# Attention row maxima: for 5 of 16 query tiles, two key blocks share one maximum through their difference

## The reference, cut to what matters

```python
# (2, 2048, 256); 16 heads of width 16
Q = (x @ WQ + bQ).reshape(b, n, N_HEADS, D_K)
K = (x @ WK + bK).reshape(b, n, N_HEADS, D_K)
V = (x @ WV + bV).reshape(b, n, N_HEADS, D_K)
Qr = jnp.einsum('bnhd,dr->bnhr', Q, WQr)
Kr = jnp.einsum('bnhd,dr->bnhr', K, WKr)
scores = jnp.einsum('bnhr,bmhr->bnhm', Qr, Kr) / math.sqrt(RANK)
A = jax.nn.softmax(scores, axis=-1)
out = jnp.einsum('bnhm,bmhv->bnhv', A, V).reshape(b, n, d)
return out @ WO + bO
```

## Time and profile before

| | |
|---|---|
| Time, median of 3 runs | 2819.9 us (2819.66 to 2824.02) |
| Time of the profiled execution | 2823.65 us |
| Its span | 2821.7 us |
| Attention in the span | about 124 to 1476 us |
| Busy: PE, DVE, ACT | 2386.1, 2258.6, 1691.3 us |

### The profile page before, as it was taken

One profiled execution on the slowest core, in us unless ns is written; L12 is line 12 of the kernel. 1 busy time (PEld: TensorE's weight loads), 2 busy tenths in 40 slices (PEclk: granted clock), 3 DMA queues, 4 the chain that ended last, 5 costly groups with the idle time before them and its releaser, 6 DMA issues. The chain is left out here.

```text
span 2821.7 us, 45555 instructions
## 1 busy us (share of the span) xinstructions
PE 2386.1 (85%) x14814; PEld 1060.6 (38%) x14814; DVE 2258.6 (80%) x3705; ACT 1691.3 (60%) x3462; POOL 961.9 (34%) x729
## 2 busy tenths in 40 slices
PE   8898999999999999999986799917476676679991
PEld 5322222222222222222225478812122222357881
DVE  7898999999999999999924844428799999785443
ACT  3347888888888888888881433306556556443330
POOL 4500000000000000000020277772499999426772
PEclk9879999999999999999997799957799999879996
DMA  4505111111111111111145469981234333245997
GB/s 152 145 24 177 43 34 50 50 36 40 50 50 36 40 50 50 32 44 50 28 132 186 142 162 270 234 124 28 55 112 113 105 112 110 85 142 153 272 239 204
DMA packets 255163, 293.69 MB, mean 104 GB/s; under 512 B 39120, under 2 KB 210448, under 8 KB 254928
## 3 DMA queue, kind: packets, MB, share of 16 engines
q1 hardware_dynamic: 213664, 235.09, 28.7%
q0 software_dynamic: 33104, 46.42, 8.9%
q10 hardware_dynamic: 8160, 9.32, 1.0%
HBM read 223.35 MB, written 66.75 MB: 103 GB/s over the span
## 5 line engine op out<-in xcount | busy, mean ns | idle before, releaser
L746 DVE TENSOR_REDUCE att_mx<-att_pR 128x1 f32<-128x512 f32 x2048 | 1266.2, 683 | 32.7 <-PE att_pR L786 32.7
L729 ACT ACTIVATE att_probs<-att_pS 128x512 f32<-128x512 f32 x2048 | 1064.0, 603 | 230.1 <-PE att_pS L816 229.9
L833 PE MATMUL att_pA<-att_probs,att_vh 128*17 128x512 f32 x4096 | 539.1, 598 | 12.6 <-ACT att_acc_sb L710 12.2
L816 PE MATMUL att_pS<-att_q,att_k 64*128 64x512 bf16 x1344 | 458.4, 379 | 0.6 <-DMA att_q<-att_nmT 0.4
L2299 PE MATMUL sc_pY<-sc_hc,all_ident 128*128 128x512 f32 x512 | 261.1, 634 | 126.9 <-DVE sc_hc L2256 102.8
L2165 POOL TENSOR_TENSOR sc_bh<-ssm_du,sc_b 128x1024 f32<-128x1024 f32 x128 | 297.7, 2358 | 8.9 <-DVE sc_hc L2256 4.7
L673 POOL TENSOR_TENSOR att_neg<-att_mx,att_minus 128x16 f32<-128x16 f32 x32 | 7.1, 221 | 842.4 <-DVE att_mx L754 842.4
L786 PE MATMUL att_pR<-head_k,head_q 64*128 64x512 bf16 x704 | 257.7, 403 | 14.3 <-PEq L72 7.4
L816 PE MATMUL att_pS<-head_q,head_k 64*128 64x512 bf16 (+1 forms) x1408 | 263.6, 380 | 0.2
L816 PE MATMUL att_pS<-att_qs,att_ks 64*128 64x512 bf16 x1344 | 260.6, 377 | 0.3
L786 PE MATMUL att_pR<-att_ks,att_qs 64*128 64x512 bf16 x672 | 259.3, 386 | 0.0
(11 more groups left out here) (320 smaller groups left out, 3595.7 us busy)
## 6 DMA issues: line engine op xcount, KB each, us to landing
sc_b<-scan_rows SPq DMA_DIRECT2D x128, 256.0 KB
f_wgu<-in_w_gate SPq DMA_DIRECT2D x128, 192.0 KB
f_wgu<-in_w_up SPq DMA_DIRECT2D x128, 192.0 KB
expert_sum<-att_zeros SPq DMA_DIRECT2D x4, 4224.0 KB, 21.2
f_wd<-in_w_down SPq DMA_DIRECT2D x128, 128.0 KB
sc_c<-scan_rows SPq DMA_DIRECT2D x40, 256.0 KB
head_q<-query_parts SPq DMA_DIRECT2D x132, 64.0 KB, 2.2
head_k<-key_parts SPq DMA_DIRECT2D x132, 64.0 KB, 2.2
```

The source lines that it names most:

```text
L729: act.activation(probs[:, k % (2 * HALF), :], bank(place(k)), ACT.Exp, scale=float(DK) ** -0.5).then_inc(expd, 1)
L746: dve.tensor_reduce(mx4[s][:, k // QC, k % QC:k % QC + 1], pR[:, (s + k) % 3, :], AX.X, ALU.max).then_inc(maxed, 1)
L816: mm = pe.matmul(bank(place(k)), kk[rows, t * P:(t + 1) * P], q[rows, c * GROUP:(c + 1) * GROUP], start=not half, stop=bool(half))
L833: mm = pe.matmul(pA[32 * c:32 * c + DK + 1, :], vh[s][:, t, :], probs[:, (HALF * g + j) % (2 * HALF), :], start=(t == 0), stop=(t == KT - ...
```

## The change

For five query tiles of each head (`FOLDED`: 1, 4, 7, 10 and 13), the key blocks 2 and 3 share one reduction. The idea is max(a, b) = b + max(a - b, 0). PE makes the difference a - b by adding two products in one bank of `pS`: the scores with block 2, and the scores with the negated block 3 (`fold_score`). ACT writes max(a - b, 0) into one of two tiles `diff` in SBUF (`rise`). Three turns later the row score b is made as before, and DVE adds the difference and takes the maximum in one `tensor_tensor_reduce`. The row score a is not made any more. POOL makes the negated key block `nk` of each head when its keys have come (`negate_keys`).

The difference takes a place in the ring of `pS`. `PLACES` is now 70, and the bank depends on the head. The difference is made at the end of turns 48, 60, 8, 20 and 32 (`TURN_OF`), and the row score is left out in turns 54, 2, 14, 26 and 38.

For head 0 all 32 pairs of key blocks are folded, blocks 0 and 1 and blocks 2 and 3 of each tile. POOL negates its two key blocks first of all, ahead of the identity matrix and the constants, and PE waits for both. The maxima of head 0 are now turned after four row steps of head 1 instead of before them.

The core of the diff (line numbers of after.py appear in the orders further down):

```diff
-    LEFT_OUT = (16, 32, 44)
-    PLACES = STEPS + 1 + len(LEFT_OUT)
+    R_RING, DIFFS = 3, 2
+    FOLDED, BEFORE = (1, 4, 7, 10, 13), QC
+    TURN_MAXIMA = QC
+    TURN_OF = {(QC * t - BEFORE - LEAD) % STEPS: t for t in FOLDED}
+    PLACES = STEPS + 1 + len(FOLDED)
...
+        def items(n):
+            return [k for k in range(STEPS) if (k // QC, (k % QC) // 2) not in folds(n) or k % 2]
...
         def place(k):
-            return k + sum(k >= left for left in LEFT_OUT) + (k >= SIDE)
+            return k + sum(k >= turn + 2 for turn in TURN_OF) + (k >= SIDE)
...
+            def negate_keys(n, s, turn):
+                pool.wait_ge(qk_in[s], 16 * LOADS * (turn + 1))
+                if n == 0:
+                    pool.tensor_tensor(nk_first[MAX_ROWS:P, :], k2[s][MAX_ROWS:P, GROUP:2 * GROUP],
+                                       minus[MAX_ROWS:P, 0:1].to_broadcast([MAX_ROWS, GROUP]), ALU.mult)\
+                        .then_inc(nk_ready, 1)
+                pool.tensor_tensor(nk[s][:, :], ks[s][0:MAX_ROWS, 3 * GROUP:4 * GROUP],
+                                   minus[0:MAX_ROWS, 0:1].to_broadcast([MAX_ROWS, GROUP]), ALU.mult)\
+                    .then_inc(nk_ready, 1)
...
+            def rise(n, t, h, scores):
+                i = folds_before(n, t, h)
+                act.wait_ge(diff_scored, i + 1)
+                if i >= DIFFS:
+                    done_n, done_t, done_h = fold_of(i - DIFFS)
+                    act.wait_ge(maxed, items_before(done_n, QC * done_t + 2 * done_h + 1) + 1)
+                act.activation(diff[i % DIFFS][:, :], scores, ACT.Relu).then_inc(diff_ready, 1)
...
+                        if k - 1 in TURN_OF and folded_at(n, k - 1):
+                            rise(*folded_at(n, k - 1), 1, bank(n, place(k) + 1))
...
+                        dve.wait_ge(diff_ready, f + 1)
+                        dve.wait_ge(row_scored, i + 1)
+                        dve.tensor_tensor_reduce(out=diff[f % DIFFS][:, :], in0=pR[:, i % R_RING, :],
+                                                 in1=diff[f % DIFFS][:, :], op0=ALU.add, op1=ALU.max, scale=1.0,
+                                                 scalar=NEG, accum_out=to).then_inc(maxed, 1)
...
+            def fold_score(n, s, t, h, scores):
+                pe.wait_ge(nk_ready, n + 2)
+                q, kk, at, less = (qs[s], ks[s], 0, nk[s]) if h else (q2[s], k2[s], MAX_ROWS, nk_first)
+                rows = q[at:at + MAX_ROWS, t * P:(t + 1) * P]
+                pe.matmul(scores, rows, kk[at:at + MAX_ROWS, 2 * h * GROUP:(2 * h + 1) * GROUP], start=True, stop=False)
+                pe.matmul(scores, rows, less[at:at + MAX_ROWS, :], start=False, stop=True).then_inc(diff_scored, 1)
...
+                        if k in TURN_OF and rows:
+                            free_bank(n, place(k + 1) + 1)
+                            fold_score(n_r, s_r, TURN_OF[k], 1, bank(n, place(k + 1) + 1))
```

More of the change, by code:

```diff
@@ L515, in phase_attention @@
         mx4 = [m.sb(f"mx4{s}", [P, KT, QC]) for s in range(SLOTS)]
+        diff = [m.sb(f"diff{s}", [P, BANK]) for s in range(DIFFS)]
+        nk = [m.sb(f"nk{s}", [MAX_ROWS, GROUP], BF16) for s in range(SLOTS)]
+        nk_first = m.sb("nk_first", [P, GROUP], BF16)
         mx = m.sb("mx", [P, KT])
@@ L564, in is_head, with fold_of, folds, items_before @@
             return isinstance(n, int) and n == k
+        def fold_of(i):
+            n = 0
+            while i >= len(folds(n)):
+                i -= len(folds(n))
+                n += 1
+            return (n, *folds(n)[i])
         def start(n):
             return is_head(n, 0)
+        def folds(n):
+            return [(t, h) for t in range(KT) for h in range(2)] if n == 0 else [(t, 1) for t in FOLDED]
+        def items(n):
+            return [k for k in range(STEPS) if (k // QC, (k % QC) // 2) not in folds(n) or k % 2]
+        def items_before(n, k=0):
+            return sum(len(items(i)) for i in range(n)) + sum(i < k for i in items(n))
+        def folds_before(n, t=0, h=0):
+            return sum(len(folds(i)) for i in range(n)) + sum(f < (t, h) for f in folds(n))
+        def early_folds():
+            return [(t, h) for t, h in folds(1) if QC * t - BEFORE < LEAD]
         def place(k):
-            return k + sum(k >= left for left in LEFT_OUT) + (k >= SIDE)
+            return k + sum(k >= turn + 2 for turn in TURN_OF) + (k >= SIDE)
         SIDE_PLACE = place(SIDE) - 1
         STEP_AT = {place(k): k for k in range(STEPS)}
-        def bank(at):
-            return pS[:, at % RING, :]
-        NT = bank(SIDE_PLACE)[0:SHIFT_ROWS * KT, 0:P]
+        FOLD_AT = {place(turn + 1) + 1: turn for turn in TURN_OF}
+        assert len(set(STEP_AT) | set(FOLD_AT) | {SIDE_PLACE}) == PLACES
+        def folded_at(n, turn):
+            ahead = 1 + (turn + LEAD) // STEPS
+            return (n + ahead, TURN_OF[turn]) if n + ahead < NH else None
+        def bank(n, at):
+            return pS[:, (n * PLACES + at) % RING, :]
+        def turned_bank(n):
+            at = (n - 1) * PLACES + SIDE_PLACE if n else RING - 1
+            return pS[0:SHIFT_ROWS * KT, at % RING, 0:P]
+        def first_bank(i):
+            return pS[:, i % (RING - 1), :]
         def load_rows(eng, n, s, side, first):
@@ L648, in _ @@
         def _(pool):
+            def negate_keys(n, s, turn):
[7 more added lines that the diff above has]
+                    .then_inc(nk_ready, 1)
+            pool.memset(minus[:, :], -1.0).then_inc(minus_ready, 1)
+            pool.wait_ge(minus_ready, 1)
+            negate_keys(0, 0, 0)
+            pool.wait_ge(nk_ready, 2)
             make_identity(pool, identb[:, :], consts, 0)
@@ L695, in head @@
                     pool.wait_ge(biased, GROUPS)
+            negate_keys(1, 1, 0)
             fetch(0, 0)
@@ L728, in head @@
                         act.wait_ge(col_scored, v(STEPS * n + k + 1))
-                        act.activation(probs[:, k % (2 * HALF), :], bank(place(k)), ACT.Exp,
+                        act.activation(probs[:, k % (2 * HALF), :], bank(n, place(k)), ACT.Exp,
                                        scale=float(DK) ** -0.5).then_inc(expd, 1)
+                        if k - 1 in TURN_OF and folded_at(n, k - 1):
+                            rise(*folded_at(n, k - 1), 1, bank(n, place(k) + 1))
                         if k == SIDE + 1 and ahead >= 1:
                             send(n + 1, (s + 1) % SLOTS, turn)
-            send(0, 0, 0, first=True)
+            for i, (t, h) in enumerate(folds(0)):
+                rise(0, t, h, first_bank(i))
+            for t, h in early_folds():
+                if t == FOLDED[1]:
+                    send(0, 0, 0, first=True)
+                rise(1, t, h, first_bank(folds_before(1, t, h)))
             heads(act, head)
@@ L800, in free_bank @@
                     pe.wait_ge(expd, v(STEPS * n_before + STEP_AT[before] + 1))
+                elif folded_at(n_before, FOLD_AT[before]):
+                    pe.wait_ge(diff_ready, folds_before(*folded_at(n_before, FOLD_AT[before]), 1) + 1)
                 else:
@@ L815, in col_half @@
                 rows = slice(at, at + (MAX_ROWS, REST_ROWS)[half])
-                mm = pe.matmul(bank(place(k)), kk[rows, t * P:(t + 1) * P],
+                mm = pe.matmul(bank(n, place(k)), kk[rows, t * P:(t + 1) * P],
                                q[rows, c * GROUP:(c + 1) * GROUP], start=not half, stop=bool(half))
```

77 lines of the change are left out of this document (51 added, 26 removed).

## The result

The changed kernel takes 2845.74 us (median of 4 runs, 2842.51 to 2848.30) against 2820.77 us for the kernel before (4 runs). The ratio is 1.0082, with a 95% interval of 1.0069 to 1.0095: slower, by about 25 us where +20 was forecast. The profiled execution took 2848.3 us.

The account below looks back on a forecast made before the run. PE and DVE were taken as nearly full, each with 0.08 us slack per group, and PE without a free place. Loop +30.9, head 1's keys -0.9 and head 0 -10 gave +20 us: 2840 us, range 2812 to 2862.

Parts of the forecast that it names:

- The loop, +30.9: Loop of the heads: groups with a difference lengthen, those with a left-out row score shorten; sum +30.9 us.
- so turns 20 and 60 pay nothing: Loop, turns 20 and 60: the wait for the pS bank, until 1.30 us, adds nothing to the group.
- The left-out rows, -0.08 each: Loop groups without r2, the left-out row score: r3's wait goes, -0.08 us, four per head, -9.9 us in all.
- Turn 8, nothing: Group of turn 8: values wait for the drain until 2.92 us, covering 2.87; nothing for 30 heads, +0.4 for head 0.
- Head 0, -10: Start of the attention: the loop starts earlier with head 0's pairs folded; -10 us, bounds -8 and -13.
- so two places: Head 0: a pair's three matmuls take two places in PE's array, 0.86 us at 1.2 GHz, so PE sets the pace.
- the -12.5: Head 0: if PE's clock rises to 2.4 GHz, the loop starts near 160.5 us, 12.5 us earlier.
- Head 1's keys, -0.9: Head 1: PE's 6.5 us wait for keys shrinks by what most of a head grows, -0.9 us.
- DVE as the bound: Rival, loop and head 0: every left-out reduction counts, 93 us and 10 in head 0, giving 2717 us; chance 5%.
- One place for the difference: Rival, loop: the difference costs one array place, not two; the sum is -6 us, 2814 us; chance 17%.
- the gains that were to cancel the cost: Rival: head 0 gives -13 or more, turn 48 is covered, some ACT waits vanish; 2825 us; chance 5%.
- The slow sum with a maximum: Rival, DVE: the sum takes over 1.4 us and delays the next r2; at 1.6 us, 2871 us; chance 10%.

Follow-up runs that it names:

- run 3: The changed kernel with one matmul for each difference in the loop, the product with the negated keys left out: 2845.96 us, ratio 1.0080.
- Run 5: The changed kernel with no differences, relus or left-out rows in the loop; only the pS ring still skips its places: 2856.60 us, ratio 1.0107.
- Run 6: The changed kernel with the difference made two turns later, at its group's end just ahead of the values: 2843.84 us, ratio 1.0066.
- run 4: The changed kernel with differences still made in the loop but not read, and all 64 rows reduced: 2857.42 us, ratio 1.0116.
- run 8: The changed kernel with nine tiles (7 to 15), one-matmul differences placed in pR, four diff tiles, no skipped pS places: 2813.39 us, ratio 0.9958.
- run 9: As run 8, but with eight folded tiles (8 to 15), without tile 7: 2811.82 us, ratio 0.9955.
- run 10: As run 8, but with only four folded tiles (8, 10, 12 and 14): 2854.11 us, ratio 1.0100.
- run 1: The changed kernel with only head 0 folded; no folded tile in the loop and no pS places skipped for folds: 2812.29 us, ratio 0.9961.
- run 7: As Run 6, but with one matmul per loop difference, by a key-block difference that GpSimd makes in bfloat16: 2817.49 us, ratio 0.9977.

## Why the prediction was right, and where it was not

**The total: partly luck.** For the attention, +20.0 us had been forecast, and +19.9 were found. But the loop with head 1's keys cost 34.0 where 30.0 had been forecast, and the part ahead of the loop gave 14.1 where 10 had been forecast. The two misses cancel.

**The loop, +30.9: size of the groups right, its cause half right.** Forecast for the groups with a difference were 2.82 (turns 20 and 60) and 2.87 (turns 32 and 48), and 2.39 for those without r2; measured are 2.82, 2.88 and 2.39 to 2.41. The step that was only half right is "so turns 20 and 60 pay nothing". The wait for the bank of `pS` was found and put at 1.30 us, which is what the rows show, but it was taken as lying under the two places, so that only the places had a price. Runs 3 and 5 show that the wait alone makes 2.82. Run 6 shows that the two places alone make it as well. Two costs of the same length covered each other, and either one gave the number.

**The left-out rows, -0.08 each.** Right: four per head, 2.39 or 2.41, and run 4 takes exactly these back. DVE had time to spare: its idle time ahead of reductions rose from 32.7 to 132.4 us.

**Turn 8, nothing.** Right: 2.92 before and after.

**The tail.** Missed: heads 30 and 31 cost 3.3 us, where some 0.4 had been forecast. The ring skips its places there too, where no difference is made. The groups of turns 48 and 60 of head 30, and of turns 20, 32, 48 and 60 of head 31, took 1.96 to 2.39 us before and take 2.81 to 2.87 now. Run 5, in which nothing but the skipped places is left, has the same 2.81 to 2.87 there.

**Head 0, -10.** The direction was right and the size was off: -14.1 at the loop's start. The step that failed is "so two places" for a pair, with "so PE sets the pace". The pairs use the halves of the array by turns: a difference by the upper half is followed by one by the lower half, and they run side by side. The matmuls of the changed kernel behind its first one, which starts at 126.40, and two windows with the columns of the earlier trace rows, one at either level of the clock:

```profile
126.41 0.60 PE L885 MATMUL att_pR<-head_k,head_q 64*128 64x512 bf16 x1
126.78 0.63 PE L894 MATMUL att_pS<-att_nk_first,head_q 64*128 64x512 bf16 x1
126.81 0.63 PE L893 MATMUL att_pS<-head_k,head_q 64*128 64x512 bf16 x1
127.21 0.63 PE L885 MATMUL att_pR<-head_k,head_q 64*128 64x512 bf16 x1
127.24 0.63 PE L894 MATMUL att_pS<-att_nk,head_q 64*128 64x512 bf16 x1
127.64 0.63 PE L893 MATMUL att_pS<-head_k,head_q 64*128 64x512 bf16 x1
...
126.40:131.40 5.00, 5.00 (x22) 1.96 (x23) 2.95 (x9) 3.22 (x6) 4.62 (x7) 0.50 0.49 141
132.40:146.40 14.00, 14.00 (x61) 5.24 (x60) 12.89 (x39) 11.71 (x21) 8.00 (x9) 1.00 0.12 35
```

From 126.40 to 127.64 two pairs took three places, 0.62 us a pair at 1.2 GHz (0.50) and not 0.86. The sums with a maximum (L839) started 0.72 us apart there (128.19 to 131.07, four pairs) and 0.71 apart after the clock had risen to 2.4 GHz (1.00). 32 pairs of 0.71 us in place of 0.86 make 4.8 us, about what the loop's start came ahead of the 163.7 forecast. The rise of the clock, to which the prediction gave 3 us, gave almost nothing. The Trainium skill ("TensorE: Matmul & The Clock Gate", Part 1) says that activity releases the full clock, and the two windows agree; the -12.5 that had been worked out by this rule lay nearer to the -14.1, but not for its reason.

What sets the 0.71 us is a ring again, the two tiles `diff`:

```profile
140.81 0.38 PE L894 MATMUL att_pS<-att_nk_first,head_q 64*128 64x512 bf16 x1
...
141.83 1.21 ACT L787 ACTIVATE att_diff<-att_pS 128x512 f32<-128x512 f32 x2 [0.21 <-PE att_pS L894]
...
142.46 0.69 DVE L839 CUSTOM_DVE_ANT_0 att_diff<-att_pR,att_diff 128x512 f32<-128x512 f32 x1
...
143.07 0.08 DVE L839 DVE_READ_ACCUMULATOR2_ANT att_mx<- 128x1 f32 x1
...
143.25 1.21 ACT L787 ACTIVATE att_diff<-att_pS 128x512 f32<-128x512 f32 x2 [0.22 <-PE att_pS L894]
```

The difference whose second matmul started at 140.81 got its relu only at 141.83, 1.02 us later; in the first pairs, at half the clock, 0.67 us were enough. That line holds two relus of 0.60 us, one behind the other. The first is followed at 142.46 by the sum with a maximum, whose second instruction ends at 143.15, and 0.10 us later the relu two pairs on begins in the same tile: 1.42 us for two pairs. (The profile names PE as what released it. `rise` waits for the tile as well, and all relus of head 0 from the third on start 0.09 to 0.13 us after the end of that second instruction two pairs earlier.) Runs 8 to 10, with four tiles and one matmul for a difference, had pairs of 0.61 us although the clock stayed at 0.50 there (126.3 to 147.5 us in run 8). No run changed the number of tiles alone.

**Head 1's keys, -0.9.** The number fits, but these runs cannot show that it does so for its reason. PE's wait fell from 6.51 to 4.76 us, the group with it from 10.23 to 9.33, and the next group took 0.46 more. In run 1, where no group of the loop grows, the group with the wait took 9.31 as well, and in the other runs between 7.95 and 10.72.

**The rivals.** DVE as the bound falls by run 4. One place for the difference falls as a forecast of this kernel by the group of 2.82, but run 7 shows its price, 2.61, once there is one matmul. Of the gains that were to cancel the cost only head 0's came. The slow sum with a maximum is refuted by its rows in the changed kernel (ns min/median/max):

```profile
L839 DVE CUSTOM_DVE_ANT_0 att_diff<-att_pR,att_diff x187: 682/687/693, 128.2 to 1439.6; 128x512 f32<-128x512 f32 x187
L839 DVE DVE_READ_ACCUMULATOR2_ANT att_mx<- x187: 82/83/85, 128.8 to 1440.2; 128x1 f32 x187
```

The first instruction takes as long as a plain reduction. The second takes 0.08 us and starts together with the next sum where DVE has no pause, so that two sums lie 0.61 us apart in run 8, and two plain reductions 0.60.

**The best versions.** Run 1 (2812.29), run 8 (2813.39) and run 9 (2811.82) beat the kernel before by 0.4 to 0.5%, and the changed one by more; they do not differ from each other by more than their intervals. Run 1 is the simplest. Two steps were not tried: run 1 with the four tiles and the one matmul of run 8's head 0, which took 2.8 us less there, and folding all sixteen tiles through `pR`, so that no group has four rows and a difference.

## What to carry to other kernels

A buffer that is taken from a ring costs twice: the work that fills it, and the wait that it brings nearer for everyone behind it in the ring. Look for the place in the program where a ring may skip for nothing (here a group's end, ahead of the values), and take one cost away at a time: with two of equal length over each other, taking away either alone shows nothing. Look at the number of buffers before the clock or the engine: in head 0, by the trace, two tiles held the pace at 0.71 us a pair, and a doubled clock gave nothing. An engine that is 98% busy may still have nothing to give; the wait that ends last tells what its relief is worth, here 0.08 us per row where an instruction costs 0.60.
